# Graph network kernel, second attention: accumulators leave PSUM through ScalarE, already multiplied by their row factors, and VectorE sums six parts two units later

## What is computed

```python
def _L2_gnn_ref(x, adj, W, a1, a2, W1, b1, ...):
    Wh = jnp.einsum('nf,hfd->hnd', x, W)
    e_src = jnp.einsum('hnd,hd->hn', Wh, a1)
    e_dst = jnp.einsum('hnd,hd->hn', Wh, a2)
    e = jax.nn.leaky_relu(e_src[:, :, None] + e_dst[:, None, :], ALPHA)
    e = jnp.where(adj[None] > 0, e, NEG)
    att = jax.nn.softmax(e, axis=-1)
    h = jnp.einsum('hnm,hmd->hnd', att, Wh)
    h = jax.nn.elu(h)
    ...
```

## Times and profile before

| | us |
|---|---|
| median of 3 runs | 4621.47 (4621.46 to 4624.59) |
| profiled execution, its own time | 4627.39 |
| span of that execution (first to last instruction) | 4625.3 |
| PE busy in the span | 3600.6 (78%) |
| DVE busy | 3656.5 (79%) |
| ACT busy | 2520.6 (54%) |

### The profile page before, as it was taken

One profiled execution on the slowest core, in us unless ns is written; L12 is line 12 of the kernel. 1 busy time (PEld: TensorE's weight loads), 2 busy tenths in 40 slices (PEclk: granted clock), 3 DMA queues, 4 the chain that ended last, 5 costly groups with the idle time before them and its releaser, 6 DMA issues. The chain is left out here.

```text
span 4625.3 us, 57062 instructions
## 1 busy us (share of the span) xinstructions
PE 3600.6 (78%) x20004; PEld 2088.3 (45%) x20004; DVE 3656.5 (79%) x6017; ACT 2520.6 (54%) x2957; POOL 1393.1 (30%) x1400
## 2 busy tenths in 40 slices
PE   4897888959997447899874475898887687888887
PEld 3587888624443123344432232576663332333333
DVE  4499999679999984499999845698884329999986
ACT  3366556348998872299898711354442234444442
POOL 0344100006997981179989700000000000000000
PEclk9998899979998769999997797999998897888888
DMA  5411000221210002411100044000001311111110
GB/s 191 160 44 28 25 30 20 76 74 46 58 39 21 7 5 90 131 44 41 39 14 7 6 142 146 20 17 15 18 10 32 127 68 39 41 57 41 46 41 14
DMA packets 162771, 239.81 MB, mean 52 GB/s; under 512 B 86225, under 2 KB 95328, under 8 KB 156784
## 3 DMA queue, kind: packets, MB, share of 16 engines
q1 hardware_dynamic: 149808, 197.90, 13.2%
q0 software_dynamic: 12656, 37.95, 2.2%
HBM read 170.30 MB, written 65.43 MB: 51 GB/s over the span
## 5 line engine op out<-in xcount | busy, mean ns | idle before, releaser
L1392 DVE SCALAR_TENSOR_TENSOR junk<-expd,mid 128x2048 bf16<-128x2048 f32 x440 | 1036.1, 2355 | 14.0
L516 ACT ACTIVATE steepz<-s1b,thr_h 128x1024 bf16<-128x1024 f32 (+1 forms) x768 | 665.6, 926 | 553.6 <-DVE mask L599 473.1
L659 PE MATMUL acc<-V,mask 128*128 128x198 bf16 (+1 forms) x5504 | 757.8, 277 | 192.0 <-DVE mask L601 192.0
L659 PEld LDWEIGHTS acc<-V,mask 128*128 128x128 bf16 x5504 | 487.1, 100 | 252.8 <-DVE mask L601 152.1
L1294 ACT ACTIVATE junk_s<-expd,nmid 128x2048 bf16<-128x2048 f32 x264 | 528.4, 2001 | 102.2 <-POOL nmid L1352 93.9
L1297 ACT ACTIVATE junk_s<-expd,nmid 128x2048 bf16<-128x2048 f32 x264 | 528.1, 2000 | 0.0
L1733 PE MATMUL psS<-KT,qs 64*128 64x512 f32 x1024 | 383.2, 740 | 156.7 <-DVE m L1843 152.2
L666 PE MATMUL acc<-V,adjT 128*128 128x99 bf16 (+1 forms) x5504 | 455.7, 221 | 0.0
L599 DVE TENSOR_TENSOR mask<-steepz,adjT 128x1024 bf16<-128x1024 bf16 (+1 forms) x768 | 397.6, 552 | 29.4 <-PE acc L659 14.9
L666 PEld LDWEIGHTS acc<-V,adjT 128*128 128x128 bf16 x5504 | 371.4, 100 | 51.5 <-issue 3.3
L1336 POOL TENSOR_SCALAR part<-signs,nmid 128x1 f32<-128x1 f32 x264 | 309.2, 1171 | 167.8 <-ACT junk_s L1297 147.1
(11 more groups left out here) (260 smaller groups left out, 5876.7 us busy)
## 6 DMA issues: line engine op xcount, KB each, us to landing
rows<-in_adj_dram SPq DMA_DIRECT2D x32, 1024.0 KB
s1b<-sT_dram SPq DMA_DIRECT2D x32, 512.0 KB, 4.1
block<-adj_dram SPq DMA_DIRECT2D x32, 512.0 KB, 4.4
adj_dram<-adjT POOLq DMA_DIRECT2D x4, 2048.0 KB, 20.5
rel_table<-zeros POOLq DMA_DIRECT2D x64, 128.0 KB, 19.8
y_dram<-yo SPq DMA_DIRECT2D x32, 256.0 KB, 2.1
yt<-y_dram SPq DMA_DIRECT2D x32, 256.0 KB, 2.9
adjT<-adj_dram SPq DMA_DIRECT2D x4, 2048.0 KB
```

The source lines that it names most:

```text
L516: act.activation(steepz[:, m % RELUS, :], s1b[:, q % 4, :], ACT.Relu, bias=thr_h[:, u, 1, j:j + 1], scale=STEEP).then_inc(relu_ready, 1)
L659: mm = pe.matmul(acc[:, c % 2, i // TB, o:o + 2 * W], mask[:, j % RING, tile(i)], V[:, u, j, 0:2, :].rearrange("p s w -> p (s w)"), start= ...
L1392: link(dve.scalar_tensor_tensor(junk[:, :], e, col(mid, i), e, ALU.is_gt, ALU.mult, accum_out=col(mass, i)))
```

## The change

In the second attention (`SCALED`, where `IB` is 4), ScalarE runs a new function `weigh` for each unit. It waits for the unit's accumulators, multiplies each of the 4 row tiles' two halves (195 columns) by its row factor into `scaled` in SBUF, eight instructions in all, and then releases the accumulators. It waits for its own writes and signals VectorE with a copy of one column (`tick`). On ScalarE this stands behind the Relu of `j` = 13 of the next unit. `results` on VectorE becomes one reduction over the six parts of `scaled`, the reciprocal and the product. It stands behind the mask of `j` = 1, two units after the one it finishes (`BEHIND` = 2), so that the last two units' results stand behind the loop.

```diff
+        SCALED = IB == 4
+        BEHIND = 2 if SCALED else 1
...
                                act.activation(steepz[:, m % RELUS, :], s1b[:, q % 4, :], ACT.Relu,
                                               bias=thr_h[:, u, 1, j:j + 1], scale=STEEP
                                               ).then_inc(relu_ready, 1)
+                                if SCALED and j == 13 and (not first or q >= 1):
+                                    weigh(h0 + u if c >= 1 else h0 + u - 1, (c - 1) % NC, h0 * NC + q - 1,
+                                          None if first and q < 2 else h0 * NC + q - 1)
+
+                def weigh(h, c, n, used):
+                    act.wait_ge(acc_ready, n + 1)
+                    if used is not None:
+                        act.wait_ge(scaled_read, used)
+                    for i in range(IB):
+                        for half, row in enumerate((g.rowE, g.rowF)):
+                            ins = act.activation(scaled[:, i, 3 * half:3 * half + 3, :].rearrange("p r c -> p (r c)"),
+                                                 acc[:, c % 2, i, half * W:(half + 1) * W], ACT.Copy,
+                                                 scale=row[:, bass.ds(h, 1), c * IB + i:c * IB + i + 1]
+                                                 .rearrange("p o t -> p (o t)"))
+                            if i == IB - 1 and half == 1:
+                                ins.then_inc(acc_free, 1)
+                    act.wait_ge(acc_free, n + 1)
+                    act.copy(tick[:, :], g.rowE[:, 0, 0:1]).then_inc(scaled_ready, 1)
...
+                if SCALED:
+                    weigh(H - 1, NC - 1, H * NC - 1, H * NC - 1)
...
                 def results(h, c, n):
 
+                    if SCALED:
+                        dve.wait_ge(scaled_ready, n + 1)
+                        dve.tensor_reduce(num[:, :, :], scaled[:, :, :, :].rearrange("p i r c -> p i c r"), AX.X,
+                                          ALU.add).then_inc(scaled_read, 1)
+                        dve.wait_ge(scaled_read, n + 1)
+                        link(dve.reciprocal(rec[:, :], num[:, :, DH]))
+                        link(dve.tensor_tensor(hid[:, c * IB:(c + 1) * IB, bass.ds(h * DH, DH)], num[:, :, 0:DH],
+                                               rec[:, :].unsqueeze(2).to_broadcast([P, IB, DH]), ALU.mult))
+                        return
...
-                                if j == RING + 1 and (not first or q >= 1):
-                                    hh = h0 + u if c >= 1 else h0 + u - 1
-                                    results(hh, (c - 1) % NC, h0 * NC + q - 1)
+                                if j == (1 if SCALED else RING + 1) and (not first or q >= BEHIND):
+                                    hh = h0 + u if c >= BEHIND else h0 + u - 1
+                                    results(hh, (c - BEHIND) % NC, h0 * NC + q - BEHIND)
...
-                results(H - 1, NC - 1, H * NC - 1)
+                for c in range(NC - BEHIND, NC):
+                    results(H - 1, c, (H - 1) * NC + c)
```

More of the change, by code:

```diff
@@ L449, in attention_stage @@
             num = self.sb(st, "num", [P, IB, C])
+            scaled = self.sb(st, "scaled", [P, IB, 2 * 3, C]) if SCALED else None
+            tick = self.sb(st, "tick", [P, 1])
+            scaled_ready = self.sem(st, "scaled_ready")
+            scaled_read = self.sem(st, "scaled_read")
             rec = self.sb(st, "rec", [P, IB])
@@ L580, in body @@
                 def body(h0, first):
-                    base[0] = 0 if first else h0 * (per_loop // 2) - per_chunk
+                    base[0] = 0 if first else h0 * (per_loop // 2) - BEHIND * per_chunk
                     base[1] = 0
@@ L612, in body @@
                                                       mask[:, (j - 1) % RING, :], ALU.subtract).then_inc(other_ready, 1)
-                                if j == RING + 1 and (not first or q >= 1):
-                                    hh = h0 + u if c >= 1 else h0 + u - 1
-                                    results(hh, (c - 1) % NC, h0 * NC + q - 1)
+                                if j == (1 if SCALED else RING + 1) and (not first or q >= BEHIND):
+                                    hh = h0 + u if c >= BEHIND else h0 + u - 1
+                                    results(hh, (c - BEHIND) % NC, h0 * NC + q - BEHIND)
                     return base[1]
-                per_chunk = 4
+                per_chunk = 2 if SCALED else 4
                 per_head = 2 * 6 + per_chunk * NC
-                in_first = 2 * per_head - per_chunk
+                in_first = 2 * per_head - BEHIND * per_chunk
                 per_loop = 2 * per_head
```

## The result

The changed kernel takes 4637.16 us (median of 11 runs, 4634.0 to 4642.43), the kernel before 4623.85 us (11 runs, 4619.55 to 4626.16). The ratio is 1.0031, with a 95% interval of 1.0022 to 1.0040: **slower by 0.3%**, 13 to 14 us, where +6.3 us was forecast and 4617 to 4635 given as the range. Of the 9.4 us between the forecast of 4627.8 and the measured time, 2.4 are of the base: the kernel before had a median of 4621.5 us over three runs and 4623.85 over eleven. The profiled execution took 4642.38 us, 15.0 us more than that of before.

A forecast was written before the change was run, and what follows sets the result against it. TensorE was taken to bound units inside heads, VectorE the pauses between heads. Pauses -13.2, waits +8.1, clock +9.8 and stage's end +1.6 gave +6.3 on 4621.5: 4627.8, rounded 4628 us, range 4617 to 4635.

The forecast's parts named there:

- What bounds the kernel, and the lead: Inside heads TensorE sets the pace; at heads' ends VectorE's lead rises to 5.4 us, shortening PE's pauses by 13.2 us.
- The saving of some 1.4 us in VectorE's work of a unit: Inside a head, VectorE's 12.43 us of work per unit falls by some 1.4 us through shorter results.
- The cost of the new results: On VectorE, reduction of 1560 elements 1.78 us; results 2.5 us outside the loop, 2.8 us inside.
- so I take the same rate: Assumes VectorE's strided SBUF reduction costs 1.045 ns an element like unstrided ones, since L562 reads strided at 0.49 us for 390.
- The wait at a head's start: PE waits for tile 1's complement at seven heads, 0.9 us at head 1, 1.2 in the loop: +8.1 us.
- The clock: After restarts PE runs at half speed; the new wait prolongs this slow stretch by 1.4 us a head: +9.8 us.
- The first rival: At heads' starts, a pause in the slow stretch doesn't lengthen it; -3.5 us, 4618 us; chance 0.20.
- ScalarE: In each unit, eight PSUM reads at 0.34 us take 2.7 us; VectorE doesn't wait for Relus, cost 0.
- The second rival: Relu of `j` = 14 comes late behind `weigh`, costing VectorE 1.2 us of lead per head; +17.5 us, 4639 us; chance 0.10.
- The stage's end: After PE's last matmul, ScalarE's part then VectorE's take 5.5 us instead of 3.95: +1.6 us, between +1.0 and +4.4.
- The sum: Whole kernel: -13.2 + 8.1 + 9.8 + 1.6 = +6.3 us, forecast 4627.8, rounded 4628 us.

The follow-up runs named there:

- the kernel with the bare wait: Kernel before, plus two useless VectorE reductions behind mask 1 of the first unit of each head but the first; ratio 1.0042 to the kernel before.
- e_c0_at5: Changed kernel with the results of each head's first unit behind tile 5, all others behind tile 1; ratio 0.9988 to the kernel before, median 4619.8 us.
- e_contig: Changed kernel with the six parts innermost in `scaled`, so VectorE's reduction reads without stride and ScalarE writes strided; ratio 1.0007 to the kernel before, median 4629.5 us.

## Why the prediction was wrong, point by point

- **What bounds the kernel, and the lead.** Right. Units inside a head stayed at 14.40 us. VectorE's last mask of a head came 5.3 to 5.4 us ahead of its matmul, and the pauses fell by 12.5 us where 13.2 was the term. The saving of some 1.4 us in VectorE's work of a unit didn't come: outside the loop the new results take 3.61 us (3038.44 to 3042.05) where 2.5 was forecast and the old ones took 3.95. The lead came from their place, not from less work.
- **The cost of the new results.** This is the step that failed: "so I take the same rate". The slope came from two reductions that read without a stride, and the only strided row, L562 in the earlier trace rows, reads PSUM in groups of 3. For SBUF in groups of 6 it doesn't hold: 2.87 to 2.91 us instead of 1.78. The text said that no strided read of SBUF was in the trace, but gave no upper bound for it, so the range was too narrow as well.
- **The wait at a head's start.** Place, number and cause were right. The size followed from the step above: 1.75 us at head 1 and 1.98 to 2.14 us in the loop instead of 0.9 and 1.2; 14.1 us instead of 8.1. Each wait is 0.86 us longer than forecast on average, and the missing 1.1 us of the reduction more than covers that. The forecast counted its wait from the start of the matmuls in the trace of before, the trace counts it from the end of the matmuls ahead, about 0.2 us later.
- **The clock.** The mechanism was right: the wait draws the slow stretch out, to 7.6 to 10.5 us (waits included) where 6 to 8.6 was given as the sign. The first rival (no effect of the wait) falls, by the kernel with the bare wait and by e_c0_at5, which has the same pauses as the changed kernel, hardly a wait, and 32.7 us of slow work instead of 52.1. That the size came out, +9.8 forecast and 10.3 in the stage, is in part luck: the term was worked out for waits of 0.9 to 1.2 us, and the waits were 1.75 to 2.14. With waits of 0.6 to 1.0 us, in e_contig, the clock cost (44.7 - 31.6) / 2 = 6.6 us. The Trainium skill, "TensorE: Matmul & The Clock Gate", section "What's actually happening", has it that a throttled clock is the default and that activity lifts it. The trace after agrees: restarts stood at 0.50, and the full clock came 2.8 to 5.5 us after the wait's end, with PE at work without a break in between.
- **ScalarE.** Its instruction starts 0.31 us after the one before and lasts 0.43; 0.34 was taken. The eight took 2.6 us, the term was 2.7. The second rival, a late Relu, does not happen in the change to any effect. It appears once the results stand behind tile 5.
- **The stage's end.** +2.55 us where 1.6 was the term and 1.0 to 4.4 the range; the difference of 1.0 is again the reduction.
- **The sum.** -12.5 + 14.1 + 10.3 + 2.55 = +14.5 us, where the forecast had -13.2 + 8.1 + 9.8 + 1.6 = +6.3. With the reduction's true time put into the same working the waits would have been 7 x 1.1 = 7.7 us longer and the end 1.1: +15.1. So the one step accounts for the size of the miss. It doesn't vouch for every other term: e_contig has the reduction at the forecast's price, and its terms are -12.3 + 6.4 + 6.6 + 2.0 = +2.7, with 0.5 of rest +3.2 (its ratio says the same), where the same working had +6.3.

## What to carry to other kernels

An engine that isn't the bound inside a stage can still set the time at the stage's joints, so ask first where its lead is spent and where it is empty: work moved out of the end of a head paid 12 us, and the same work at the next head's start cost 24, because there PE had used up the ring and needed each tile as it was written. Where several instructions become one, look at how that one reads: price a reduction by a row with its own memory, stride and group length, or lay the data out so that it reads contiguously. And place work for a restart of TensorE so that no wait falls into the slow stretch behind it.

## What the runs showed of the hardware that was not expected

- A reduction of fp32 on VectorE from SBUF costs 2855 ns for 1560 elements in groups of 6 with a stride of 65 elements, against 1778 contiguous; from PSUM 390 elements in groups of 6 with that stride cost 566 ns, from SBUF 836.
- A ScalarE instruction from PSUM to SBUF that writes 195 fp32 elements 24 bytes apart lasts 0.60 us, a contiguous one 0.43.
- A wait of 1.6 us in the slow stretch behind a restart cost the stage 3.2 us, half of it by the clock. Waits of 1.6 to 1.9 us at full clock were followed by a slow stretch of 3.4 us in three cases of seven.
- With PE's pause 0.8 us shorter, the full clock came only 0.2 us sooner after PE's stop in one kernel, and the slow work of the whole stage was 8.5 us more; in another kernel with shorter pauses still it was only 1.1 us more. What decides that was not tested.
